# Attention values in two column tiles of TensorE, row sums partly on POOL and DVE

## The reference

```
x = x + cross_attention(layernorm(x), ctx)             # 8 heads of 32, 77 keys
x = x + ternary_ffn(layernorm(x))                      # 256 -> 1024 -> 256, 8-bit activations
x = x + attention(queries = layernorm(x),              # 4 heads of 64, RMS-normed q and k,
                  keys = [layernorm(x), ctx], mask)    # 1024 + 77 keys, ctx keys masked
x = x + moe(layernorm(x))                              # 8 experts, top 2, and a shared expert
```

```
p = exp(q . k - max);   o = (p @ v) / sum(p);   x += o @ Wo[h]
```

## Time and profile before

| | us |
|---|---|
| median of 3 runs | 1007.7 |
| the runs | 1012.25, 998.62, 1007.7 |
| the profiled execution | 1010.25 |
| its span | 1008.5 |

### The profile page before, as it was taken

How to read it: one execution, slowest core, us unless ns; L and a number is a source line. 1 busy time by engine, 2 the same in 40 slices (tenths; PEclk the granted TensorE clock), 3 DMA queues, 4 the chain that set the end, 5 groups by cost and what they waited for, 6 DMA issues and landing times.

```text
span 1008.5 us, 15098 instructions
## 1 busy us (share of the span) xinstructions
PE 915.3 (91%) x4323; PEld 639.1 (63%) x4327; DVE 663.0 (66%) x1310; ACT 511.8 (51%) x816; POOL 388.7 (39%) x314
## 2 busy tenths in 40 slices
PE   8986767988999999999999999779999999999991
PEld 3643444554455555555556678567888888788881
DVE  4576997776555765765469577775666666566666
ACT  2334776545456556546543432313666666566660
POOL 1013441544444664664514676851232232222210
PEclk9787998999999999999999999989999999999995
DMA  9200000002855955965881500009661077617214
GB/s 300 72 1 0 1 0 1 1 1 77 308 194 188 362 221 181 354 231 185 333 340 67 219 1 1 1 16 388 243 265 36 31 288 307 266 36 281 81 48 167
DMA packets 49079, 153.62 MB, mean 152 GB/s; under 512 B 6145, under 2 KB 23610, under 8 KB 43408
## 3 DMA queue, kind: packets, MB, share of 16 engines
q1 hardware_dynamic: 45296, 143.83, 38.3%
q0 software_dynamic: 3744, 9.31, 2.9%
HBM read 97.55 MB, written 56.49 MB: 153 GB/s over the span
## 4 chain that ended last, share of the span: by engine, by line
PE 67%; DVE 17%; DMA 4%; issue 4%; ACT 3%; POOL 3%; SPq 0%; DVEq 0%; ACTq 0%; POOLq 0%
PE banks L967 13%; PE banks L1204 6%; PE banks L1206 6%; PE banks L1205 6%; PE banks L959 4%; PE banks L935 3%; PE banks L978 3%; PE banks L960 3%; DMA aux<-moe_x,small 3%; PE banks L876 2%; PE banks L1229 1%; PE banks L1231 1%; PE banks L1230 1%; PE banks L1072 1%; DVE small L1790 1%
## 5 line engine op out<-in xcount | busy, mean ns | idle before, releaser
L967 PE MATMUL banks<-wexp 128*65 128x512 f32 (+1 forms) x288 | 149.5, 600 | 2.2 <-ACT wexp L1482 2.0
L610 POOL TENSOR_TENSOR cv_hl<-wexp,cv_hl 128x1024 fp32r<-128x1024 f32 x45 | 109.0, 2433 | 70.3 <-ACT cv_hl L1468 70.3
L1204 PE MATMUL banks<-ring,x_hi 128*128 x312 | 128.2, 411 | 0.0
L1482 ACT ACTIVATE wexp<-banks 128x512 f32<-128x512 f32 x128 | 76.1, 601 | 97.1 <-PE banks L960 96.9
L1206 PE MATMUL banks<-ring,x_lo 128*128 x312 | 122.5, 393 | 0.0
L1205 PE MATMUL banks<-ring,x_hi 128*128 x312 | 122.5, 393 | 0.0
L1909 DVE TENSOR_REDUCE small<-banks 128x1 f32<-128x1101 f32 x64 | 83.5, 1304 | 51.7 <-PE banks L936 51.7
L1595 ACT ACTIVATE banks<-wexp 128x1024 f32 x72 | 73.4, 1020 | 47.7 <-DVE aux L2257 47.7
L959 PE MATMUL banks<-q_hi,k_hl 128*128 128x512 f32 x144 | 86.4, 600 | 1.7 <-ACT q_lo L1459 1.0
L1578 ACT ACTIVATE aux<-banks 128x512 f32<-128x512 f32 x78 | 46.7, 599 | 67.1 <-PE banks L1206 47.8
L1206 PEld LDWEIGHTS banks<-ring,x_lo 128*128 128x128 f32 x312 | 59.0, 189 | 13.1
(11 more groups left out here) (343 smaller groups left out, 2253.0 us busy)
## 6 DMA issues: line engine op xcount, KB each, us to landing
wsplit<-cv_hl SPq DMA_DIRECT2D x45, 1024.0 KB, 7.6
ring<-wsplit SPq DMA_DIRECT2D x32, 1280.0 KB, 13.2
wexp<-in_L_ffn_w SPq DMA_DIRECT2D x40, 512.0 KB, 5.5
wexp<-in_expert_biases SPq DMA_DIRECT2D x8, 1152.0 KB, 6.6
ring<-wsplit SPq DMA_DIRECT2D x4, 1024.0 KB, 9.0
wexp<-moe_y SPq DMA_DIRECT2D x8, 512.0 KB, 6.7
wexp<-in_L_ffn_sw SPq DMA_DIRECT2D x5, 512.0 KB, 11.3
x_sb<-in_x SPq DMA_DIRECT2D x4, 512.0 KB, 7.6
```

What stands on the lines that cost most here:

```text
L610: g.tensor_tensor(sides(hl[:, PIECE:2 * PIECE]), raw, sides(hl[:, 0:PIECE]).bitcast(f32), ALU.subtract).then_inc(s['cv_lo'], 1)
L967: mm(pb[5 + half][0:DA, :], vh[b][0:w, c, :], pT[q % 3][0:w, :], start=c == 0, stop=c == len(KTILES) - 1).then_inc(s['a_pv'], 1)
L1204: mm(o[:], x_hi[u][:, kc, :], hi, start=kc == 0 and not primed, stop=False, skip_group_check=primed)
L1482: a(pT[q % 3], pb[3 + q % 2][:], ACT.Exp).then_inc(s['a_p'], 1)
```

## The change

The ones column of `vh` goes; values have 64 stationary columns. Both halves of a block are computed one after the other, the first into partitions 0 to 63 of bank 5, the second into partitions 64 to 127 of bank 6, once both probabilities are there: block 0 at q = 3, blocks 1 to 7 at every second q from 4 to 16, block 8 behind the last q. The probabilities get ten tiles (five for each half). POOL adds blocks 1 to 3 onto block 0 (six instructions a step, one pair behind each of its first three conversions), DVE adds blocks 5 and 6 onto block 4 (four, behind its negated maxima; in step 0 mostly among the maxima, in step 7 behind its roots and among the tokens it normalises). PE then sums blocks 0, 4, 7 and 8 over the keys with a stationary tile of ones, 32 columns wide: for each half two matmuls before and two behind the values of block 8, into the partitions of banks 5 and 6 that the values leave free. The joins take all 128 rows of `oT`, with 1 in Wo's added column at rows 64 and 96.

ACT's copies of the outputs move from the end of a step to q = 1 of the next and become three; its roundings of weights move to other q, its reuse of a probability tile waits for POOL's or DVE's add. The bias table moves to words that are free from the start; POOL zeroes it among its constants, SP loads it right behind its first loads, POOL splits it in the first stage, and ACT waits for that before step 0. The diff, cut (`...`):

```diff
-        vh = [scr.take((TB + 1) * DA, TB + 1) for _ in range(2)]
-        pT = [scr.take(512) for _ in range(3)]
+        vh = [scr.take((TB + 1) * DH, TB + 1) for _ in range(2)]
+        p_tiles = [scr.take(512) for _ in range(4)]
...
+        ax.at = 0
+        p_tiles += [ax.take(512) for _ in range(4)]
+        ax.at = kept_to
+        p_tiles += [ax.take(512) for _ in range(2)]
+        bias_f = wexp[:, 0:NB]
+        bias_part = wexp[:, NB:NB + NB // 2].bitcast(bf16)
...
-        CONV_AT = (1, 4, 7, 9, 12, 14)
+        CONV_AT = (4, 7, 9, 11, 13, 17)
         CONV_END = (0, 2, 4)
         PER_STEP = len(CONV_AT)
+        TAKEN = (0, 2, 3, 4, 1, 2, 3, 4, 2)
+        P_TILE = [[p_tiles[2 * k + half] for half in range(2)] for k in TAKEN]
+        FIRST_SUM, SECOND_SUM, SINGLE = 0, 4, 7
+        ADDS, ADDS5, SUMS = 2 * 3, 2 * 2, 4 * 2
...
-            link(g.memset(woT[DH:DA, :, 0:D], 0.0))
-            link(g.memset(woT[DH:DA, :, D:D + 1], 1.0))
+            link(g.memset(woT[DH:P, :, :], 0.0))
+            for row in (DH, DH + 32):
+                link(g.memset(woT[row:row + 1, :, D:D + 1], 1.0))
+            g.memset(bias_f, 0.0).then_inc(s['r_zero'], 1)
             g.iota(eno_i[:], pattern=[[0, 1]], base=0, channel_multiplier=1).then_inc(s['const'], 1)
             flat = lambda v: v.rearrange("p a b -> p (a b)")
-
+            NU = 2 * (TB + 1)
+
+            pool.wait_ge(s['ld_route'], NLD['ld_route'])
+            part = bias_part[0:96, :]
+            for k in range(3):
+                link(g.tensor_copy(part, bias_f[0:96, :]))
+                link(g.tensor_copy(bias_b[32 * k:32 * k + 32, :], part[32 * k:32 * k + 32, :]))
+                if k < 2:
+                    link(g.tensor_tensor(bias_f[0:96, :], bias_f[0:96, :], part, ALU.subtract))
+            pool.sem_inc(s['r_bias'], 1)
...
-            pool.wait_ge(s['l_free'], 1)
-            g.memset(bias_f, 0.0).then_inc(s['r_zero'], 1)
-
-            def head(n, h, b):
-                pool.wait_ge(s['a_o'], n - 1)
-                head_values(h, b)
-                pool.wait_ge(s['a_hi'], n * 5 + 5)
-                head_keys(b)
...
+            def add(n, c):
+
+                for half in range(2):
+                    pool.wait_ge(s['a_p'], n * NU + 2 * c + half + 1)
+                    if c == 1:
+                        pool.wait_ge(s['a_pv'], n * NU + 2)
+                    else:
+                        pool.wait_ge(s['a_add'], n * ADDS + 2 * (c - 2) + half + 1)
+                    acc = P_TILE[FIRST_SUM][half]
+                    g.tensor_tensor(acc, acc, P_TILE[c][half], ALU.add).then_inc(s['a_add'], 1)
...
             for p in range(PER_STEP):
                 conv(p)
-                if p == PER_STEP // 2 - 1:
+                if p < 3:
+                    add(0, p + 1)
+                if p == 1:
                     pool.wait_ge(s['a_hi'], 10)
                     head_keys(1)
-            PARTS = 3
-            part = bias_part[0:96, :]
             for i in range(NH - 1):
                 for b in range(B):
-                    head(i * 2 + (2 + b), i + 1, b)
+                    n = i * 2 + b + 1
+                    pool.wait_ge(s['a_o'], n)
+                    head_values(i + 1, b)
                     for p in range(PER_STEP):
-                        conv((i * 2 + b + 1) * PER_STEP + p)
-                for k in range(PARTS)[i::NH - 1]:
-                    if k == 0:
-                        pool.wait_ge(s['ld_route'], NLD['ld_route'])
-                    link(g.tensor_copy(part, bias_f[0:96, :]))
-                    link(g.tensor_copy(bias_b[32 * k:32 * k + 32, :], part[32 * k:32 * k + 32, :]))
-                    if k < PARTS - 1:
-                        link(g.tensor_tensor(bias_f[0:96, :], bias_f[0:96, :], part, ALU.subtract))
+                        conv(n * PER_STEP + p)
+                        if p < 3:
+                            add(n, p + 1)
+                        if p == 0:
+                            pool.wait_ge(s['a_hi'], n * 5 + 10)
+                            head_keys(b)
             for p in range(PER_STEP * (B * NH - 1), CONV):
                 conv(p)
-            pool.sem_inc(s['r_bias'], 1)
+                add(B * NH - 1, p % PER_STEP + 1)
...
-            def values(n, b, q):
-                c, half = divmod(q, 2)
-                a, w = KTILES[c]
-                pe.wait_ge(s['a_p'], n * NU + (q + 1))
-                mm(pb[5 + half][0:DA, :], vh[b][0:w, c, :], pT[q % 3][0:w, :], start=c == 0,
-                   stop=c == len(KTILES) - 1).then_inc(s['a_pv'], 1)
+            def values(n, b, c):
+
+                w = KTILES[c][1]
+                pe.wait_ge(s['a_p'], n * NU + (2 * c + 2))
+                if c == 0 and (not isinstance(n, int) or n > 0):
+                    pe.wait_ge(s['a_o'], n)
+                for half in range(2):
+                    mm(pb[5 + half][half * DH:(half + 1) * DH, :], vh[b][0:w, c, :], P_TILE[c][half][0:w, :], start=c == 0,
+                       stop=c == len(KTILES) - 1).then_inc(s['a_pv'], 1)
+
+            def sums(pair, begins):
+
+                for half in range(2):
+                    for k, c in enumerate(pair):
+                        w, row = KTILES[c][1], (1 - half) * DH + k * 32
+                        mm(pb[5 + half][row:row + 32, :], ones[0:w, 0:32], P_TILE[c][half][0:w, :], start=begins, stop=not begins)\
+                            .then_inc(s['a_sum'], 1)
+
+            def added(n):
+                pe.wait_ge(s['a_add'], n * ADDS + ADDS)
+                pe.wait_ge(s['a_add5'], n * ADDS5 + ADDS5)
+                sums((FIRST_SUM, SECOND_SUM), True)
...
-                    if q == 0 and not first:
-                        pe.wait_ge(s['a_o'], n)
-                    values(n, b, q)
+                    if q == 3:
+                        values(n, b, 0)
+                    elif q % 2 == 0 and q > 2:
+                        values(n, b, q // 2 - 1)
...
-                    out_q = q - (2 if last else 5)
+                    out_q = q - (4 if last else 5)
...
+                added(n)
+                values(n, b, TB)
+                sums((SINGLE, TB), False)
...
+            def outputs(n, b):
+
+                act.wait_ge(s['a_pv'], n * NU)
+                act.wait_ge(s['a_sum'], n * SUMS)
+                a(oT[b][:, 0:512], pb[5][:], ACT.Copy)
+                a(oT[b][0:DH, 512:S], pb[6][DH:P, :], ACT.Copy)
+                a(oT[b][DH:P, 512:S], pb[6][0:DH, :], ACT.Copy).then_inc(s['a_o'], 1)
...
-                    if q >= 3 or not first:
-                        act.wait_ge(s['a_pv'], n * NU + (q - 2))
+                    if q == 0 and not first:
+                        act.wait_ge(s['a_sum'], n * SUMS - SUMS // 2)
+                    if half == 0 and 5 <= c < TB:
+                        act.wait_ge(s['a_pv'], n * NU + 2 * (c - 3))
+                        act.wait_ge(s['a_add'], n * ADDS + 2 * (c - 4))
+                    if q == 2 * TB:
+                        act.wait_ge(s['a_pv'], n * NU + 2 * 6)
+                        act.wait_ge(s['a_add5'], n * ADDS5 + 2)
                     if q < 2 * TB:
-                        a(pT[q % 3], pb[3 + q % 2][:], ACT.Exp).then_inc(s['a_p'], 1)
+                        a(P_TILE[c][half], pb[3 + half][:], ACT.Exp).then_inc(s['a_p'], 1)
                     else:
-                        a(pT[q % 3][0:SK, :], pb[3 + q % 2][0:SK, :], ACT.Exp, bias=mask_col[:, b:b + 1]).then_inc(s['a_p'], 1)
+                        a(P_TILE[c][half][0:SK, :], pb[3 + half][0:SK, :], ACT.Exp, bias=mask_col[:, b:b + 1]).then_inc(s['a_p'], 1)
+                    if q == 1 and not first:
+                        outputs(n, 1 - b)
...
-                act.wait_ge(s['a_pv'], n * NU + NU)
-                a(oT[b][0:DA, 0:512], pb[5][0:DA, :], ACT.Copy)
-                a(oT[b][0:DA, 512:S], pb[6][0:DA, :], ACT.Copy).then_inc(s['a_o'], 1)
+                if last:
+                    outputs(n + 1, b)
...
+            def add(n, c, half):
+
+                ve.wait_ge(s['a_p'], n * NU + 2 * c + half + 1)
+                if c == SECOND_SUM + 1:
+                    ve.wait_ge(s['a_pv'], n * NU + 2 * (SECOND_SUM + 1))
+                else:
+                    ve.wait_ge(s['a_add5'], n * ADDS5 + half + 1)
+                acc = P_TILE[SECOND_SUM][half]
+                v.tensor_tensor(acc, acc, P_TILE[c][half], ALU.add).then_inc(s['a_add5'], 1)
...
+                    if first and t in (4, 5, 6):
+                        add(n, 5, t - 4) if t < 6 else add(n, 6, 0)
                 if not last:
                     minus(n + 1)
+                    if not first:
+                        add(n, 5, 0)
+                        add(n, 5, 1)
+                        add(n, 6, 0)
+                    add(n, 6, 1)
...
-            v.tensor_copy(mx4[:, 1:2], f_max[:, 0:1]).then_inc(s['l_free'], 1)
...
-            for t in range(TB):
+            for half in range(2):
+                add(HEADS - 1, 5, half)
```

(38 more changed lines are left out.)

## The result

The changed kernel takes 1037.65 us (median of 1028.81, 1042.02, 1037.11 and 1038.2) against 1007.4 for the kernel before on the same chip: a ratio of 1.032, 95% interval 1.026 to 1.038. It is slower. The time lies in the forecast's range, but the forecast's case was "no change".

What follows compares the result with a forecast made beforehand. PE's program order was taken to bound the attention, with DVE's turns of the maxima and ACT's list at a step's start behind it. 1010.25 - 9 + 0.6 + 5 = 1006.9 us, as a median 1004; range 978 to 1048.

Steps and rivals of the forecast that it cites:

- the forecast's case: Whole kernel: the tiles of a pair overlap fully, median 1004 us, no change that can be told; chance 0.40.
- passes in order: Rival, values on PE: passes start in program order, a pair takes 1.29 us, median 1046 us; chance 0.30.
- Overlap: Values on PE: the two tiles of a pair overlap fully, 9 pairs of 0.86 us, 7.7 us less a step.
- no overlap: Rival, values on PE: a pair stays 1.72 us, step 46.8 us, median 1091 us; chance 0.10.
- wrong if a pair takes over 1.0 us: Sign against the forecast, values on PE: a pair over 1.0 us, or odd turns below 2.2 us.
- Changes of the tile: PE in a middle step: nine uncovered entries cost 0 to 1.4 us, taken as 0.7.
- The maxima: Eight maxima of a middle step: turns without values held at 2.30 us by DVE, 1.2 us gained.
- Start to first maxima: Start of a middle step: ACT's list decides, gain between 0.2 and 2.6 us, taken as 1.4.
- Tail: End of a middle step: first sums wait for DVE's four adds, loss 0 to 2 us, taken as 0.4.
- Last step: Last attention step: joins start two q later, between 4 us less and 3 more, taken as nothing.
- Bias split: First stage: POOL's split delays DVE's token normalising and PE's turning, 0 to 11 us, taken as 5 more.
- the condition that I gave: DVE beside POOL: operations with two SBUF inputs wait out a POOL instruction that has begun.

Runs made afterwards that it cites:

- the control: Kernel before, without column tiles, with DVE copying the outputs and ACT's first two roundings of a step moved to q = 6: ratio 1.000 (0.997 to 1.003).
- filling the one wait: Changed kernel with 40 matmuls of no use ahead of PE's third turning of tokens: 1036.6 us, ratio 1.035 (1.030 to 1.040).

## Why the prediction was wrong

The time fell into the range by luck: its slower half was there for the rival of passes in order (1046), and that rival is not what happened.

**Overlap** was right: a pair is 1.01 us against 1.86 on the same columns, and the first passes of its two tiles start together. The rivals "passes in order" and "no overlap" fell; the second's step of 46.8 us is nearly what the tiles on one set of columns gave (45.8). The Trainium skill's rule (TensorE: Matmul & The Clock Gate, Part 3) on strict order, from which I drew a rival of three passes, doesn't forbid two passes beside each other; its speed for column tiles was the better guide. But "wrong if a pair takes over 1.0 us" was met by a hair, and it is where the sum begins to fail.

**Changes of the tile** is the mis-sized term of the middle steps: 0.7 us a step for nine entries, where each pair was measured at 0.33. For the seven pairs of a step behind its first maxima that is 2.3 us; the two others stand where PE waits for ACT. I had halved the one row that priced it, taking the late weight load out, and the late weight load is the cost. The Trainium skill (TensorEngine Tiling (Array Packing), Tiling Modes) says that a change of mode drains the engine: 0.14 on the way in and 0.19 on the way back is what the rows show of it. Two turns are 5.25 us where the sum had 2.60 and 2.30, and the 0.35 is as much as that change, 0.15 in the turn with values and 0.20 in the other. The sum also had the wait for DVE in the wrong turn: it stands ahead of the maxima of the turn with values and takes 0.27 of its 3.01. And the 2.30 of step 0 that I read as DVE's turn was PE's own order too: 0.64 and 0.14 for maxima, 0.66 for scores and 0.86 for values. The maxima lose 0.5 us a step where I had a gain of 1.2.

**Start to first maxima** went as argued, smaller: ACT's list decides, 0.6 us gained of the 1.4 that I took (0.8 to DVE's first reduction), inside its bounds. **Tail**: last maximum to first score is 8.2 us instead of 7.4 to 7.7, a loss of 0.5 to 0.8 where I had 0.4. The sums follow the pairs without a wait there, so PE does not wait for DVE's adds; the five groups of pairs and sums take 5.0 us together where the five values took 4.4, which is the changes of tile again. First maximum to first maximum a step takes 0.4 us more instead of 1.5 less. From step 0's first maximum to the last of step 6 that is 3.7 us more where I had 9 less: 12.7 us of the miss.

**Last step**, "Between 4 less and 3 more; I take nothing" and 0.6 for the third copy: 12.9 more, and 12.3 of the miss. The step that failed is that I moved the joins by two q and did not follow what stood ahead of them: copies that had ended the step before now stood in ACT's list at its start, and PE had no transposes to do meanwhile, so it waited and its clock fell. Nor did I count that sums and the pair of block 8 now come behind the tokens on PE. The joins' place cost 4.4 us in the traces with and without it; the rest is read from rows of the chain and not tested apart.

**Bias split**: the mechanism was right to the row (TENSOR_SCALARs that end with POOL's instructions, third turning 5.2 us late), and its size wrong: 16 us in medians against 5, beyond my bound of 11. I built it on one execution whose third turning came at 45.4; the same first stage had it at 41.5 in the control. In that execution PE itself was late: from 40 to 45 us its clock was 0.50, and DVE's tokens, ready at 43.2, waited for it. That hid half of DVE's delay, which is 10.2 us against the kernel without the split (50.5 and 40.3). Nor does the condition that I gave, two inputs in SBUF, cover it: a cast with one input waited as well (1.01 us instead of 0.17). What of the 16 lies in TensorE's clock in the rest of the stage stays open: filling the one wait did not return it.

The sum of these, 12.7 + 12.3 + 11, is 36 us, against the 33.6 by which the median was missed; the first two are from single traces, the third from medians, so it is a rough check.

## What to carry to other kernels

Column tiles save PE's passes, but each change of tile shape, there and back, cost a third of a microsecond here; group work of one shape, and count both ways. When PE's share of a step shrinks, list the next engine's whole sequence at the place where PE will wait, and relieve it in the same change: here the tiles alone lost, relief alone gave nothing, and both together, with scores regrouped and the bias split cut up, gained a third of a percent. Put long POOL instructions with SBUF operands nowhere near a DVE chain, or cut them up.

## What the runs showed of the hardware

A DVE operation that waits for POOL waits not only for the instruction that has begun: where the next followed without a gap it waited out both (4.78 us). It need not be large either: casts of 128x8 took 1.01 us instead of 0.17 while POOL added. And two column tiles of float32, two passes with a weight load each, lay fully beside each other: four passes in 1.01 us. What they cost is the weight loads at either end, 0.14 and 0.19 us, which stood behind passes as long as the shape did not change.
